# GpSimd's drain left out of the block ends, and attention's first tiles of x asked for ahead of its tables, in a three-layer transformer kernel

## What is computed

```python
x = x + 0.5 * ffn(layernorm(x))       # 32 experts, best 6 per token, at most 192 tokens each, plus a shared expert
x = x + attention(layernorm(x))       # 4 query heads on one key/value head, RMS norm with gains, rotary positions
x = x + 0.5 * ffn(layernorm(x))
```

## Time and profile before

| | us |
|---|---|
| median of 3 runs | 1692.7 (1690.84 to 1692.87) |
| the profiled execution's own time | 1691.99 |
| its span, from the program's first to its last instruction | 1690.2 |
| outside the span | 1.8 |
| first expert block | 218.4 to 549.5 |
| attention | 549.5 to 1160.1 |
| second front | 1160.1 to 1369.5 |
| second expert block | 1369.5 to 1690.2 |

### The profile page before, as it was taken

One profiled execution on the slowest core, in us unless ns is written; L12 is line 12 of the kernel. 1 busy time (PEld: TensorE's weight loads), 2 busy tenths in 40 slices (PEclk: granted clock), 3 DMA queues, 4 the chain that ended last, 5 costly groups with the idle time before them and its releaser, 6 DMA issues. The chain is left out here.

```text
span 1690.2 us, 26016 instructions
## 1 busy us (share of the span) xinstructions
PE 1483.3 (88%) x8434; PEld 1232.9 (73%) x8436; DVE 1112.2 (66%) x2284; ACT 1028.2 (61%) x2108; POOL 767.1 (45%) x659
## 2 busy tenths in 40 slices
PE   5999969899994589999999999995999869999994
PEld 4877758777773477887887887774887758778773
DVE  4659857777773256666666675664649857777773
ACT  5762447777773266666667666753762537777773
POOL 0123235555653475666556556420113225556563
PEclk9999979999998789999999999997999989999998
DMA  7736358889994111111111110115655448999994
GB/s 268 239 128 205 107 187 267 253 256 259 266 253 79 64 39 51 38 38 63 38 44 45 63 38 32 32 38 179 212 175 158 139 152 255 269 255 266 268 258 72
DMA packets 94599, 255.57 MB, mean 151 GB/s; under 512 B 19153, under 2 KB 20113, under 8 KB 86193
## 3 DMA queue, kind: packets, MB, share of 16 engines
q1 hardware_dynamic: 71984, 202.58, 35.8%
q0 software_dynamic: 22528, 51.92, 14.4%
HBM read 185.70 MB, written 68.76 MB: 151 GB/s over the span
## 5 line engine op out<-in xcount | busy, mean ns | idle before, releaser
L1032 DVE TENSOR_TENSOR e_w_lo<-e_raw,e_w_hi 128x1024 fp32r<-128x1024 f32 x192 | 233.6, 1218 | 108.7 <-ACT e_w_hi L947 100.5
L947 ACT ACTIVATE e_w_hi<-e_raw 128x1024 fp32r<-128x1024 f32 x192 | 202.6, 1056 | 29.2 <-PEq L270 20.8
L1548 POOL TENSOR_SCALAR t_prob<-t_prob,t_inv 128x128 f32<-128x128 f32 (+7 forms) x128 | 112.0, 875 | 221.7 <-DVE t_inv L1455 221.7
L1122 PE MATMUL e_ps_gate<-e_xt,e_w_hi 128*128 128x384 f32 x512 | 161.3, 378 | 38.6 <-DVE e_w_lo L1032 38.5
L899 POOL DMA_INDIRECT e_xg<-htab,e_gather_idx x128 | 140.0, 1093 | 63.5 <-issue 39.3
L910 POOL DMA_INDIRECT x_after_ffn<-e_y,e_add_idx x64 | 104.4, 1631 | 114.8 <-DMA x_after_ffn<-e_y,e_add_idx 92.1
L910 POOL DMA_INDIRECT out<-e_y,e_add_idx x64 | 104.7, 1637 | 104.3 <-DMA out<-e_y,e_add_idx 83.8
L1122 PE MATMUL e_ps_up<-e_xt,e_w_hi 128*128 128x384 f32 x512 | 151.8, 361 | 0.0
L353 POOL TENSOR_SCALAR d_inter<-d_inter 128x512 f32<-128x512 f32 x32 | 26.5, 827 | 267.8 <-DVE d_inter L518 267.6
L1350 ACT ACTIVATE t_prob<-a_wide,t_neg_max,a_q_scale 128x128 f32<-128x128 f32 (+7 forms) x128 | 106.5, 832 | 54.0 <-DVE t_neg_max L1449 53.8
L1122 PEld LDWEIGHTS e_ps_gate<-e_xt,e_w_hi 128*128 128x128 f32 x512 | 99.0, 193 | 48.6 <-issue 28.9
(11 more groups left out here) (222 smaller groups left out, 4476.9 us busy)
## 6 DMA issues: line engine op xcount, KB each, us to landing
e_raw<-in_w_experts SPq DMA_DIRECT2D x64, 1536.0 KB
htab<-d_h SPq DMA_DIRECT2D x16, 1024.0 KB, 5.3
d_x<-in_x SPq DMA_DIRECT2D x16, 512.0 KB, 6.8
d_xs<-in_x SPq DMA_DIRECT2D x32, 256.0 KB, 3.5
x_after_ffn<-d_xs SPq DMA_DIRECT2D x32, 256.0 KB, 3.2
q_x<-x_after_ffn SPq DMA_DIRECT2D x32, 256.0 KB, 3.1
t_res<-x_after_ffn SPq DMA_DIRECT2D x32, 256.0 KB, 2.6
x_after_attention<-t_res SPq DMA_DIRECT2D x32, 256.0 KB, 2.0
```

Source lines behind the costliest of these rows:

```text
L947: act.activation(w_hi[u][:, cols], raw[u][:, cols], ACT.Copy).then_inc(hi_ready, 1)
L1032: dve.tensor_tensor(w_lo[u][:, cols], raw[u][:, cols], w_hi[u][:, cols].bitcast(F32), ALU.subtract).then_inc(lo_ready, 1)
L1122: pe.matmul(out, w[0][:, c, cols], xt[u][:, c, :, :], start=c == 0, stop=False)
L1548: pool.tensor_scalar(prob[:, u, 0:width(i)], prob[:, u, 0:width(i)], inv[:, u:u + 1], 1.0, ALU.mult, ALU.mult).then_inc(p_ready, 1)
```

## The change

In attention SP asks for tiles 0 and 1 of x first, then for the three tables, then for the other tiles. POOL's wait for the tables moves from ahead of its loop into `gain` of tile 0.

```diff
-        with nc.Block() as block:
+        with nc.Block(no_gpsimd_drain=True) as block:
...
             @block.sync
             def _(sp):
-                for t, name in ((cos, "cos"), (sin, "sin"), (gains, "gains")):
-                    sp.dma_start(t[:, :, :], a[name]).then_inc(loaded, 16)
-
...
-                for T in range(LEAD + 2):
+                load_x(0)
+                load_x(1)
+                for t, name in ((cos, "cos"), (sin, "sin"), (gains, "gains")):
+                    sp.dma_start(t[:, :, :], a[name]).then_inc(loaded, 16)
+                for T in range(2, LEAD + 2):
                     load_x(T)
...
                     pool.wait_ge(raw_ready, T + 1)
                     if T:
                         pool.wait_ge(rot_added, T)
+                    else:
+                        pool.wait_ge(loaded, 16 * 3)
                     pool.tensor_tensor(gained[:, :, :], raw[T % 2][:, :, :], gains[:, :, :], ALU.mult)
...
-                pool.wait_ge(loaded, 16 * 3)
                 for T in STEPS:
```

## The result

The changed kernel took 1681.35 us (median of 4 runs, 1679.48 to 1682.52) against 1692.51 us before (4 runs); the ratio is 0.9923 with a 95% interval of 0.9909 to 0.9936, that is 11 to 15 us faster (the two medians differ by 11.2). The profiled execution took 1681.07 us over a span of 1679.3 us; 1.8 us lie outside the span, as before. So the forecast of 1677 us, with a range of 1674 to 1685, held in sign and range, and was 4.4 us too low.

The account below looks back on a forecast made before the run. Joints where no engine overlaps another were taken as what counts. From 1692.0 us, 9.0 (first joint, both edits) + 6.4 (last end) + 0 (rest) = 15.4 gave 1676.6, adjusted to 1677 us; range 1674 to 1685.

Parts of the forecast that it names:

- The drain of the expert blocks, 6.4 us each: At both expert blocks' ends POOL's drain stands uncovered on the path; removing it gives at most 12.8 us per run.
- Line 1224 inherits the drain: Behind the first joint's barrier, POOL's next drain lasts 6.36 us, holding POOL alone until 550.25; total 1677 us, chance 0.40.
- The rival in which both vanish: At both expert ends the long drain is owed to no one: 10.0 + 6.4 us gained, 1675.6 us, chance 0.22.
- Tile 0 lands in 3.7 us: At attention's start, x's first tile, issued first, takes 3.7 us from issue to landing instead of 6.0; bounds 2.6 to 6.0.
- Barrier's form: At five block ends the new barrier might cost 0.3 us more each, 1.5 us in all; taken as 0.
- other three ends: At the ends of blocks other than the experts', dropping POOL's drain gives 0, because SP's stores cover it.
- tables: In attention, loading them behind tiles 0 and 1 costs 0: there by 553 us, needed at 562.7, cover 9.7 us.
- moved wait: In attention, moving POOL's wait for the tables into `gain` of tile 0 gives 0 on its own.
- The last end's gain may come back outside the span: At the last expert block's end, the drain returns on POOL before the execution ends: 1683.0 us, chance 0.24.
- "I take 0 and +-1.5 us" for the clock: Behind the shifted attention start and at later joints, TensorE's clock may rise sooner or later: 0, within +-1.5 us.
- The slower rival: In the second expert block, indirect DMAs become dearer; at 1.5 us each, 45 us longer, 1722 us, chance 0.03.

Follow-up runs that it names:

- the changed kernel's second comparison: The changed kernel run again with no edit, against the kernel before: 1677.64 us, ratio 0.991 (0.989 to 0.993).
- The kernel with 20 matmuls: The changed kernel with 20 extra matmuls of 512 columns ahead of TensorE's first real work in attention: 1679.68 us, ratio 0.9914 to the kernel before.
- memset: The kernel before, all drains kept, with one small POOL memset between its wait for all scatters and the block end's drain: 1693.29 us, one run.
- gathers only: The kernel before without the second expert block's 64 scatters and the waits for them, gathers still done: 1680.48 us, one run.
- 24 matmuls ahead and 5 in the second gap: The changed kernel with 24 extra matmuls ahead of TensorE's first transposes and 5 between the first two tiles': 1676.80 us, ratio 0.9878 to the kernel before.

## Why the prediction was right, and where it was wrong

**The drain of the expert blocks, 6.4 us each: right.** It was fully on the path and is fully gone at both: 7.0 us at the first joint and 6.38 at the end with the drains alone. Drains and order together gave 9.43 + 6.38 = 15.8 us in the places named, for 15.4 forecast; the changed kernel's second comparison gives 15 us (12 to 19), the first 13 (11 to 15).

**Line 1224 inherits the drain: wrong, by the mechanism.** It was my likeliest case. The row shows 0.210 us. The drain was taken as a debt of the scatters that someone must pay; no instruction did. An explicit drain right behind the wait is long, line 1224's, behind the branch and the barrier's semaphore instructions, is short, so the price hangs on the instruction or on its exact place, and can be left out. The rival in which both vanish, at 10.0 + 6.4 us, is what happened, with 0.6 us less for the landing.

A debt paid silently, while POOL has nothing but the 0.57 us of the clear to do for 6.5 us behind line 1224's drain in the changed kernel, would look the same there. The kernel with 20 matmuls tells: its line 1224's drain starts at 540.3, so that 6.36 us of hidden work would hold POOL until 546.6, and POOL starts at 545.47, as soon as the inverse is there:

```profile
545.18 0.17 DVE L1404 RECIPROCAL q_rstd<-q_std 128x2 f32<-128x2 f32 x1 [0.36 <-ACT q_std L1313]
545.47 2.08 POOL L1521 TENSOR_SCALAR q_h<-q_x,q_mv,q_rstd 128x512 f32<-128x512 f32 x1 [8.52 <-DVE q_rstd L1404]
```

That the forecast came close with the wrong case in it is luck in part. The inherited drain would have run beside the load of tile 0 and cost only 1.0 us of the sum (10.0 against 9.0), and tile 0 then landed 0.64 us later than forecast, so that 9.43 us were measured where 9.0 stood. With the landing as it was, an inherited drain would have held POOL for some 0.4 us only (543.7 + 6.36 + 0.03 + 0.57 + 0.1 = 550.8, against 550.44). No time could tell the two cases apart; the row of line 1224 does.

**Tile 0 lands in 3.7 us: mis-sized.** It took 4.34, and 3.63 to 4.52 in four more profiles, but 2.75, 2.81 and 2.94 in others that ask for tile 0 first. The step's direction, its bounds (2.6 to 6.0) and the tables' cost of 0 held; what seems to decide within the bounds is named below.

**Barrier's form, other three ends, tables, moved wait: 0, right.** From SP's branch at routing's end to the release there are 0.3 us as before. POOL's `gain` of tile 0 waited for ACT's unloading, not for a table, as its row of the changed kernel says, beside the earlier trace rows:

```profile
561.51 1.57 POOL L1529 TENSOR_TENSOR q_gained<-q_raw,a_gains 128x640 f32<-128x640 f32 x1 [6.93 <-ACT q_raw L1328]
```

**The last end's gain may come back outside the span: not so.** 1.7 to 1.9 us are outside in every run of every kernel. The rule of the Trainium skill, page "Runtime: NRT & Kernel Launch", section "The launch sequence", puts a barrier and the rearming of the DMA rings behind the kernel; whatever they do, no measured time here grew by it.

**The absolute number: 4.4 us low.** The sum was made on one execution whose second front had no low stretch of the clock behind its first 22 us. "I take 0 and +-1.5 us" for the clock was the step that failed: second fronts of the same kernel, before, differ by 3.6 us, first expert blocks up to POOL's branch by 4 over all kernels (322.4 to 326.5), and second ones by 6 over the thirteen with scatters (313.0 to 318.9; the kernel before has both 314.0 and 318.0). That spread is in the base as well as in the result, and +-1.5 us was too little for it. Why the four executions of the first comparison's base lay together at its low end stays open.

**The slower rival: not seen.** The scatters' median in the second expert block is 1.447 us, for 1.450 in the earlier trace rows, and the block's 315.6 us up to the branch lie between the 314.0 and 318.0 of the kernel before.

## What to carry to other kernels

A drain of GpSimd that directly follows indirect DMAs cost 5.3 to 6.5 us here, although a semaphore or 30 us of time stood for their landing; where a semaphore already says that they have, the block's end can go without it, and each such joint with nothing beside it gave the whole amount, 6.4 us. At a joint where every engine waits for one first tile, its load belongs ahead of tables that are needed 10 us later; that gave 4.6 us with all drains kept and 2.4 (9.45 to 7.04) without them. And before an absolute number is forecast from one profile, a second profile of the same kernel tells which stretches are that execution's own: the chain at the joint repeated within 0.25 us in two pairs of profiles, a stage of 200 us within 4.

## What was not expected of the hardware

**What makes the drain long is not settled.** Long, 5.3 to 6.5 us: directly behind scatters (block end or explicit), 30 us behind the last gather, and with a memset between. Short: line 1224's drain, 0.210 us, 0.3 us behind the branch that waits for the scatters, and every drain behind it, though attention's first comes only 18 us later; they add about 0.1 us to the work that they wait for. Line 1224's is the one that goes with a reset of semaphores. Whether it is short by its kind or by the barrier's semaphore instructions ahead of it, and whether these, it, the clear of the range or POOL's first normalisations end the long state, wasn't tried.

**An instruction load seems to delay the first tile.** Eight profiles have x first in SP's queue. In five of them one load of 16 KB on queue q8 began 1.1 to 2.1 us behind the release and lasted 0.93 to 1.5 us, and tile 0 took 3.63 to 4.52 us. In the other three the load lay 14 to 21 us ahead of the release, and tile 0 took 2.75 to 2.94. All eight agree, but the cause is inferred, and what moves the load was not tried. The six profiles with the tables first show no such split: tile 0 took 5.4 and 5.6 us in the two whose load lay 20 to 22 us ahead of the release (memset, gathers only), and 3.9 to 6.0 in the four with the load behind it. The Trainium skill, page "DMA: Bandwidth & Descriptors", section "Why a DMA increments its semaphore by 16 and not by 1", says that a DMA is spread over up to 16 engines and has landed only when the last of them is done; by that, one engine held by the instruction load would be enough, which these durations fit and do not prove.

**The clock fell again behind the first transposes.** With 20 matmuls TensorE idled 0.8 and 1.4 us around the first transposes, and the clock was low again for 3.4 us afterwards; with 24 matmuls ahead and 5 in the second gap, it stayed up until 17 us behind the first normalisation, and attention was 2 to 3 us shorter. Which of the two additions did it was not separated.
